# A GNN edge loop: gather waits once in eight, two steps between hand-overs, and the node update among the last groups

## The reference

```python
h = jnp.maximum(_layernorm(x, axis=-1), 0.0)
edge_in = jnp.concatenate([h[row], h[col], dist], axis=1)      # row, col, dist = src, dst, edge_weight1
e = jax.nn.silu(edge_in @ eW1 + eb1)
e = jax.nn.silu(e @ eW2 + eb2)
agg = jax.ops.segment_sum(e, row, num_segments=h.shape[0])
node_in = jnp.concatenate([h, agg], axis=1)
out = jax.nn.silu(node_in @ nW1 + nb1) @ nW2 + nb2
return x + out
```

## Time and profile before

| what | value |
|---|---|
| median of three runs | 3638.94 us |
| the profiled execution | 3647.13 us |
| its span, first to last instruction | 3645.3 us |
| mean granted TensorE clock | 0.907 |
| first stage | about 838 us |
| edge loop | 838 to about 3574 us |
| node update | about 3574 to 3645 us |

### The profile page before, as it was taken

The page is one execution under the profiler, slowest core; times in us unless marked ns, Lnnn a source line. Parts: engine busy times, 40 slices in busy tenths (PEclk is TensorE's granted clock), DMA queues, the critical chain, the costliest instruction groups (busy, mean ns, idle before and its releaser), DMA issues.

```text
span 3645.3 us, 77682 instructions
## 1 busy us (share of the span) xinstructions
PE 2686.2 (74%) x21518; PEld 2217.8 (61%) x21818; DVE 2082.7 (57%) x7353; ACT 1600.4 (44%) x3444; POOL 2023.8 (56%) x2077
## 2 busy tenths in 40 slices
PE   6998999894677677776676767777667667676668
PEld 3555555553666666666666666666666666666667
DVE  8888988864444444444444444444444444444444
ACT  4677767762333333333333333333333333333332
POOL 0354444445666666666666666666666666666660
PEclk7999999996889888888899898988989989888889
DMA  2011111112222222222222222222222222222213
GB/s 79 25 30 36 34 24 34 35 30 41 48 48 47 48 48 48 48 48 47 49 48 48 47 49 48 47 48 49 47 48 48 48 47 48 47 49 44 44 43 143
DMA packets 363356, 171.81 MB, mean 47 GB/s; under 512 B 288823, under 2 KB 329455, under 8 KB 363247
## 3 DMA queue, kind: packets, MB, share of 16 engines
q0 software_dynamic: 69664, 123.62, 13.8%
q1 hardware_dynamic: 271390, 36.35, 6.3%
q10 hardware_dynamic: 22192, 10.53, 1.0%
HBM read 139.30 MB, written 31.04 MB: 47 GB/s over the span
## 4 chain that ended last, share of the span: by engine, by line
PE 67%; issue 24%; DVE 4%; ACT 3%; another core or an unknown queue 1%; POOL 0%; DMA 0%; ACTq 0%; DVEq 0%; POOLq 0%; SPq 0%
PE bk L1210 14%; PE bk L1219 12%; PE bk L1200 10%; PE bk L1198 7%; PE bk L1188 4%; PE bk L1062 3%; PE bk L1208 2%; PE bk L1096 2%; PE bk L1128 1%; PE bk L1050 1%; PE bk L1051 1%; PE bk L1230 1%; PE bk L1277 1%; ACT BIG L1338 1%
## 5 line engine op out<-in xcount | busy, mean ns | idle before, releaser
L534 POOL DMA_INDIRECT GA<-q_d,IX x1760 | 1682.8, 956 | 1041.5 <-remote 496.9
L910 DVE TENSOR_TENSOR BIG<-bk,BIG 128x128 f32 x1760 | 512.3, 291 | 1377.1 <-PE bk L1219 738.7
L1210 PE MATMUL bk<-W,ED 128*128 128x128 f32 x3520 | 542.9, 305 | 487.6 <-issue 476.1
L1426 ACT ACTIVATE ED<-bk,eb1c 128x512 f32<-128x512 f32 x440 | 302.3, 687 | 1329.6 <-remote 1112.0
L1200 PE MATMUL bk<-OHS,P 128*128 128x128 bf16 x5280 | 640.3, 245 | 0.0
L1198 PE MATMUL bk<-identf,GA 128*128 128x128 f32 x1760 | 563.8, 320 | 79.4 <-issue 64.8
L1200 PEld LDWEIGHTS bk<-OHS,P 128*128 x5280 | 532.7, 113 | 53.9
L1210 PEld LDWEIGHTS bk<-W,ED 128*128 128x128 f32 x3520 | 543.2, 221 | 17.2
L1219 PE MATMUL bk<-ED 128*128 128x128 f32 x3520 | 526.5, 295 | 0.7 <-ACT ED L1431 0.7
L901 DVE SCALAR_TENSOR_TENSOR GA<-c_bc,EW,GA 128x128 f32<-128x128 f32 x1760 | 498.8, 344 | 10.2 <-DMA GA<-q_d,IX 10.2
L1208 PEld LDWEIGHTS bk<-B,ones 128*128 128x128 bf16 x440 | 43.3, 98 | 757.3 <-issue 746.2
(11 more groups left out here) (243 smaller groups left out, 3054.3 us busy)
## 6 DMA issues: line engine op xcount, KB each, us to landing
GA<-q_d,IX POOLq DMA_INDIRECT x1760
q_d<-QS SPq DMA_DIRECT2D x14, 448.0 KB
u_d<-QS ACTq DMA_DIRECT2D x98, 64.0 KB
P<-u_d SPq DMA_DIRECT2D x8, 768.0 KB, 11.0
rec_d<-ED SPq DMA_DIRECT2D x16, 220.0 KB, 9.3
RW<-rec_d SPq DMA_DIRECT2D x110, 32.0 KB
rec_d<-BIG,GA POOLq DMA_INDIRECT x208
HT<-hT_d ACTq DMA_DIRECT2D x99, 32.0 KB
```

The lines of the kernel that those rows point to most:

```text
L534: e.indirect_dma_start(G[k % 4 * U + u], None, q_d, bass.IndirectOffsetOnAxis(ap=IX[g // BG % 2][:, k * U + u:k * U + u + 1], axis=0))\
L910: e.tensor_tensor(AGG[:, ds(v, P)], banks[6 + k % 2][:, u * P:(u + 1) * P], AGG[:, ds(v, P)], ALU.add).then_inc(s["ad"], 1)
L1210: last = e.matmul(z[:, u * HF:(u + 1) * HF], E1[k % 2][:, u * P:(u + 1) * P], W2[:, :], start=False, stop=(u == U - 1))
L1426: e.activation(E1[k % 2], banks[2 + k % 2][:, :], ACT.Silu, bias=eb1c[:, :]).then_inc(s["e1"], 1)
```

## The change

The first 416 groups (`TAIL`) keep the loop, with another spacing. PE does mA(g), mB(g-2), mC(g-4), mD(g-6) in a step; ACT does tcopy(g-2), silu1(g-4), silu2(g-6), widen(g-5); DVE does build(g+1), add(g-7), weigh(g). The ring `OHb` has eight places. POOL waits for `z1` only at even groups, until it counts g-2 (mB of group g-3 done), and then issues eight gathers. PE's and ACT's loop bodies hold eight groups. `node_part` stands before mA on PE and after tcopy(g-2) on ACT.

At group 416 PE, ACT and DVE finish what is in flight and then go on in the old order for groups 416 to 439, with one bank per hand-over (argument `two` is 0), one POOL wait per group, and one chunk of the node update in each step from chunk 0 on: inner(c-3), hidden(c-4), the third silu(c-4), outer(c-5), bias(c-5), finish(c-6) with c = g - 415. `inner(c)` waits until the adds of all groups up to 415 + c are done. Every chunk has its own DMAs for u, x and the output; they go through four and six buffers.

```diff
@@ -41,6 +41,11 @@
+LAG = 7
+FINAL = (E // P + 3) // U
+TAIL = (FINAL + 1) // 8 * 8
+NF2 = NFC + 1
+assert E // P + NB <= NT and FINAL + NFC == NG - 1
 
...
@@ -218,13 +221,16 @@
-        OHb = [OHS[:, k * 512:(k + 1) * 512].rearrange("p (u a) -> p u a", a=P) for k in range(4)]
-        OHT = [OHS[:, 2048 + k * 512:2048 + (k + 1) * 512] for k in range(2)]
+        OHb = [OHS[:, k * 512:(k + 1) * 512].rearrange("p (u a) -> p u a", a=P) for k in range(8)]
+        OHT = [OHS[:, 4096 + k * 512:4096 + (k + 1) * 512] for k in range(2)]
+        UR = [sb("UR", [P, 512], fp32)] + [OHS[:, o:o + 1024].bitcast(fp32) for o in (5120, 2048, 3072)]
+        assert 5120 + 1024 <= 2 * HOT
+        F1 = [QSall[:, HF + k * 512:HF + (k + 1) * 512] for k in range(3)]
+        XR = [t[:, 0:4, :].rearrange("p a f -> p (a f)") for t in (XC[0], XC[1], XM, SQ, H[0], H[1])]
...
@@ -424,34 +426,53 @@
+            with e.Fori(1, TAIL // (2 * BG)) as i:
                 for k in range(2):
                     load_rec(i, k)
 
-            e.wait_ge(s["z1"], NG)
+            def load_u(c):
+
+                w, rows = size(c)
+                e.dma_start(UR[c % 4][:, 0:w], u_d[:, c * 512:c * 512 + w]).then_inc(s_fx[c % 4], 16)
+
+            def load_nodes(c):
+
+                if c >= 6:
+                    e.wait_ge(s_out[c % 6], 16 * (c // 6))
...
+                w, rows = size(c)
+                e.dma_start(XR[c % 6][0:rows, :], nodes(x, c)).then_inc(s_fy[c % 6], 16)
+
+            def store(c):
+
+                e.wait_ge(s["fo"], c + 1)
+                w, rows = size(c)
+                e.dma_start(nodes(out, c), XR[c % 6][0:rows, :]).then_inc(s_out[c % 6], 16)
+
+            left = list(range(TAIL // BG, NG // BG))
+            for b in left[:2]:
+                load_rec(b // 2, b % 2)
+            for c in range(4):
+                if c == 2:
+                    e.wait_ge(s["tp"], TAIL)
+                    e.wait_ge(s["of"], TAIL)
+                load_u(c)
+            for c in range(5):
+                load_nodes(c)
+            for b in left[2:5]:
+                load_rec(b // 2, b % 2)
+            for c in range(NF2):
+                if c + 4 < NF2:
+                    load_u(c + 4)
+                if c == 4:
+                    for b in left[5:]:
+                        load_rec(b // 2, b % 2)
+                store(c)
+                if c + 5 < NF2:
+                    load_nodes(c + 5)
+            for k in range(6):
+                e.wait_ge(s_out[k], 16 * ((NF2 - 1 - k) // 6 + 1))
...
@@ -527,8 +548,10 @@
 
                 k = g % 4
                 for u in range(U):
-                    if u == 0:
+                    if u == 0 and g >= TAIL:
                         ge(e, s["z1"], g - 3)
+                    elif u == 0 and g % 2 == 0:
+                        ge(e, s["z1"], g - 2)
                     if u == 2 and g + 1 < NG and (g + 1) % BG == 0:
                         e.wait_ge(s["ix"], (g + 1) // BG + 1)
                     e.indirect_dma_start(G[k % 4 * U + u], None, q_d,
...
 
-            def build(g, k, j=None):
+            def build(g, k, j=None, ring=8):
 
                 if j is not None:
                     e.wait_ge(s["ix"], j + 1)
-                ge(e, s["tp"], g - 3)
                 li = LI[k // BG][:, :].bitcast(fp32)
                 for u in range(U):
                     w = k % BG * U + u
-                    ins = e.tensor_scalar(OHb[k % 4][:, u, :], iob[:, :], li[:, w:w + 1], None, ALU.is_equal)
+                    ins = e.tensor_scalar(OHb[k % ring][:, u, :], iob[:, :], li[:, w:w + 1], None, ALU.is_equal)
                 ins.then_inc(s["oh"], 1)
...
             for k in range(8):
                 build(k + 1, (k + 1) % 8, (k + 1) // BG if (k + 1) % BG == 0 else None)
+                if k >= LAG:
+                    add(k - LAG, (k - LAG) % 4)
                 weigh(0, k)
-                if k >= 2:
-                    add(k - 2, k % 4)
                 if k % BG == BG - 1:
                     decode(2 + k // BG, k // BG, 1, k + 1)
-            with e.Fori(1, NG // 8 - 1) as i:
+            with e.Fori(1, TAIL // 8) as i:
                 for k in range(8):
                     build(i * 8 + (k + 1), (k + 1) % 8, i * 2 + (k + 1) // BG if (k + 1) % BG == 0 else None)
+                    add(i * 8 + (k - LAG), (k - LAG) % 4)
                     weigh(i, k)
-                    add(i * 8 + (k - 2), k % 4)
                     if k % BG == BG - 1:
                         decode(i * 2 + (2 + k // BG), k // BG, i + 1, i * 8 + (k + 1))
-            for g in range(NG - 8, NG):
+            for g in range(TAIL - LAG, TAIL - 2):
+                add(g, g % 4)
+
...
+            for g in range(TAIL, FINAL + NF2 + 6):
+                c = g - FINAL
+                if 0 <= c - 4 < NF2:
+                    hidden(c - 4)
                 if g + 1 < NG:
-                    build(g + 1, (g + 1) % 8, (g + 1) // BG if (g + 1) % BG == 0 else None)
-                weigh(g // 8, g % 8)
-                add(g - 2, (g - 2) % 4)
-            for g in (NG - 2, NG - 1):
-                add(g, g % 4)
-
+                    build(g + 1, (g + 1) % 8, (g + 1) // BG if (g + 1) % BG == 0 else None, 8 if g + 1 < TAIL + 4 else 4)
+                if g < NG:
+                    weigh(g // 8, g % 8)
+                if g - 2 < NG:
+                    add(g - 2, (g - 2) % 4)
+                if g % BG == BG - 1 and g // BG + 2 < NG // BG:
+                    decode(g // BG + 2, g // BG % 2, g // (2 * BG) + 1, g + 1)
+                if 0 <= c - 5 < NF2:
+                    bias(c - 5)
+                if 0 <= c - 6 < NF2:
+                    finish(c - 6)
...
 
-            def mA(g, k):
+            def mA(g, k, two=1):
                 e.wait_ge(s["oh"], g + 1)
-                ge(e, s["oT"], g - 1)
-                tp = TPb[k % 2]
+                ge(e, s["oT"], g - two)
+                tp = TPb[k % 2 * two]
+            def mB(g, k, two=1):
                 vs = blocks(g, mybir.EngineType.PE)
                 e.wait_ge(s["oT"], g + 1)
                 e.wait_ge(s["st"], g + 1)
-                ge(e, s["e1"], g - 1)
+                ge(e, s["e1"], g - two)
                 for u, v in enumerate(vs):
-            def mC(g, k):
+            def mC(g, k, two=1):
                 e.wait_ge(s["e1"], g + 1)
-                ge(e, s["e2"], g - 1)
-                z = banks[4 + k % 2]
+                ge(e, s["e2"], g - two)
+                z = banks[4 + k % 2 * two]
                 e.matmul(z[:, :], ones[:, :], B2[:, :, :].rearrange("p a b -> p (a b)"), start=True, stop=False)
                 for u in range(U):
...
+            def superstep(g, k, h=None):
+
+                if h is not None and k % 4 == 0:
+                    ge(e, s["oT"], g - 1)
+                    node_part(h)
+                if h is not None and k % 4 == 2:
+                    e.wait_ge(s["uc"], h + 1)
+                mA(g, k)
+                mB(g + (-2), k + 6)
+                mC(g + (-4), k + 4)
+                mD(g + (-6), k + 2)
+
+            for lo, hi in ((1, NB // 2), (NB // 2, TAIL // 8)):
                 with e.Fori(lo, hi) as i:
-                    for k in range(4):
+                    for k in range(8):
+                        superstep(i * 8 + k, k, i * 2 + k // 4 if hi == NB // 2 else None)
+            for g in range(TAIL, TAIL + 4):
+                if g < TAIL + 2:
+                    mB(g - 2, g - 2)
+                if g < TAIL + 3:
+                    mC(g - 4, g - 4)
+                mD(g - 6, g - 6)
+
...
+                w, rows = size(c)
+                e.wait_ge(s["ad"], (FINAL + c + 1) * U + 1)
+                ge(e, s["fa"], c - 1)
+                e.matmul(banks[1 + c % 2 * 2][:, 0:w], nW1b[:, :], AGG[:, c * 512:c * 512 + w], start=True, stop=True)\
+                ge(e, s["fo"], c)
+                hid = F1[c % 3][:, 0:w].rearrange("p (n j) -> p j n", j=4)
+            e.wait_ge(s["uc"], NB)
+            for g in range(TAIL, FINAL + NF2 + 5):
+                c = g - FINAL
+                if g < NG:
+                    mA(g, g % 4, 0)
+                if g - 2 < NG:
+                    mD(g - 2, (g - 2) % 4)
+                if 0 <= c - 3 < NF2:
+                    inner(c - 3)
+                if g - 1 < NG:
+                    mC(g - 1, g - 1, 1 if g == TAIL else 0)
+                if g < NG:
+                    mB(g, g % 4, 0)
+                if 0 <= c - 5 < NF2:
+                    outer(c - 5)
...
+            for lo, hi in ((1, NB // 2), (NB // 2, TAIL // 8)):
                 with e.Fori(lo, hi) as i:
+                    for k in range(8):
+                        g = i * 8 + k
+                        tcopy(g + (-2), k + 6)
+                        if k % 4 == 2 and hi == NB // 2:
+                            node_part(i * 2 + k // 4)
+                        silu1(g + (-4), k + 4)
+                        silu2(g + (-6), k + 2)
```

(23 more changed lines are left out.)

207 lines of the change are left out of this document (66 added, 141 removed).

## The result

The changed kernel takes 4015.48 us (median of six runs, 4012.04 to 4018.61) where the kernel before takes 3638.64 (six runs, 3637.64 to 3643.51): 1.103 times as long, 95% interval 1.1018 to 1.1046. The forecast was 3391 us, in a range of 3330 to 3560. The profiled execution has a span of 4016.8 us.

The account below looks back on a forecast made before the run. It took POOL's gathers plus one pause per group, not work, as the bound. Terms -230 + 18 + 14 - 50 = -248 us gave about 3399 us profiled, 3391 against the median; range 3330 to 3560.

Parts of the forecast that it names:

- What bounds the kernel: Edge loop: POOL's four gathers and one pause make the 6.13 us period; PE's later posts get through only in POOL's pauses.
- Gather waits: POOL, groups 4 to 415: one wait per two groups cuts a group from 6.178 to 5.62 us, -230 us.
- Longer release: Rival, chance 0.12: after eight gathers PE's posts come out 1.8 us late; 5.92 us a group, loop -106, 3515 us.
- Slower: Rival, chance 0.10: posts come out 3.57 us after a run of eight gathers; 6.81 us a group, 3881 us.
- The mark I had set: Sign in the profile of the changed kernel: POOL idle over 2.4 us before each eighth gather means the main term is wrong.
- Slack, order, loop bodies, node parts: Loop on PE, ACT and DVE: two-step slack, eight-group bodies and moved node parts were taken to cost 0.
- The clock: Granted clock in the loop, 0.89 before, was expected within 0.85 to 0.93 because idle is moved and not removed.
- Drain: Group 416: emptying and refilling PE's six steps in flight costs three group periods, +18 us, with 6 to 30 possible.
- Tail: Last groups with a node-update chunk in each: PE-bound or just below, 0.6 us a group over 23 groups, +14 us.
- End: From the last gather's end to the span's end: 88.6 us become 38, -50 us.
- The likeliest case's own range: Whole kernel, likeliest case 3391 us: 3350 to 3460 with drain 6 to 30, tail 0 to 57, group 5.58 to 5.68.
- Running ahead: Rival, chance 0.05: z1 of g-3 gets through during the run, POOL never pauses; 5.03 us a group, 3148 us.

## Why the prediction was wrong, point by point

**What bounds the kernel.** Right for a held chip: POOL's gathers and one pause make the period, and the pause is not PE's work. With the wait per group it came back at 6.07 us in two kernels. "The price of every wait that POOL really has to sit in" was half of it: a pause is also where PE catches up.

**Gather waits, -230 us.** Wrong, +408.8, and this is the step that failed: "it holds only if PE can do two groups from one pause to the next with posts delivered in the pause alone". I set PE's 8.6 us of work against 11.2 us and never asked whether PE works while its posts are held. It does for about 6 us of a run of eight, then at one matmul per 0.72 or 1.41 us. So of two groups the last mB is left for the pause. 9.8 + 1.8 + 2.4 = 14.0 for one pair, 2 x 7.18 = 14.4 on average, where 11.16 was forecast. Of the 2.87 us that this pair is over the forecast, the later release is 0.62 (1.81 for 1.19), the mB left over 2.17 (2.40 for the 0.23 from silu to gather), and the run itself 0.08. The rows of before could not show this: in the steady state PE had to wait for a silu first, and in the first groups, with twenty gathers end to end, it had little to do and did it at its pace. It was an assumption that needed a reason or a price, and had neither. That posts come out "in the pause alone" was too strong as well: at 2513.49 one came through in the run.

**Longer release (0.12).** Its straight line from 1.19 (four) to 3.57 (twenty) gave 1.8 us for eight: measured 1.81. By itself it would have made 5.92 a group. **Slower (0.10)** had the pair at 13.54 us and 3881 us in all, by a release of 3.57; the time came nearest to it and went past, but by another road: 1.81 us of release and, for the larger part, unfinished work. That 4015 lies near this rival's 3881 is luck. The mark I had set, idle before each eighth gather over 2.4 us, was met with 4.2 to 5.1.

**Slack, order, loop bodies, node parts: 0.** Right: the kernel with the wait per group has all of them and 6.07 us. Code packets rose from 51 to 64 on one queue over the span, none of them in the loop between 1000 and 3600 us, so there was no reload. The clock was not within 0.85 to 0.93 but 0.78, as an effect of the run of eight (0.91 in the same order with runs of four).

**Drain, +18.** Measured +11.5, of which some 4 us are the slower loop of its first groups. **Tail, +14.** Measured +10.8 on the held chip; PE is the bound there or just below it, as I had it, with 105.73 of 113 us busy. **End, -50.** Measured -51.0 from the first silu of group 439. My own measure was another: from the last gather's end (3970.40) to the span's end there are 46.4 us, where I had 38 and before has 88.6, so -42; on that measure the tail costs 2 us and not 11. The two together, -36 forecast and -40 measured, are right.

**The likeliest case's own range.** Its terms (drain 6 to 30, tail 0 to 57, group 5.58 to 5.68) add up to 3349 to 3471, not 3350 to 3460. Nothing hangs on it.

**Running ahead (0.05).** It is what free chips do: POOL never pauses and a group takes 5.01 us. I had 5.03 for it, as a rare case of the change. It is not the change that brings it, but the chip: the old order with its wait thinned out has 5.01 us there too, in the same time as the kernel before.

## What to carry to other kernels

When an engine's signals come late, look in the trace whether the engine itself still works at its pace in that time; "done but not told" and "not done" look the same at the waiting engine and cost very differently when the interval is stretched. A wait that costs a pause may also be what gives another engine its turn: price a removal by what the others did in that pause. And before tuning an interplay of this kind, time it on several chips: here one wait was worth 398 us on one chip and nothing on another, while the overlap of the node update with the last groups gave 0.9% on free chips, and on a held one 0.9% together with the new order.

## What the hardware showed that I had not expected

- The same program takes 3110 to 3121 us on five chips and 3592 to 3639 us on others. The 1.25 us per gather is the same on both, and POOL's 0.95 us of it too; a post of PE is answered within 0.10 us on the one and comes over a microsecond behind a run of gathers on the other. What makes a chip one or the other, and what in a gather PE stands behind, stays open.
- A gather of 64 rows costs POOL 1.22 us where one of 128 costs 1.25; a plain DMA of 128 rows on the same queue costs 0.53.
- On held chips PE's matmuls themselves slow down to one per 0.72 or 1.41 us, though they wait for no semaphore: some 6 us into a run of eight gathers, some 4 us into a run of four, and not at all in the kernel before, where PE has less to issue behind a held post.
